# A per-sample 3x3 convolution on Trainium2: mixing every sample's taps from whole float32 weights instead of from weights split in two float16 parts

## The reference

```python
pooled = jnp.mean(x, axis=(2, 3))
att = sigmoid(pooled @ att_w.T + att_b)              # 16 samples x 4
agg_w = jnp.einsum('nk,kocij->nocij', att, weight)   # per sample 256 x 256 x 3 x 3
out = vmap(conv)(groupnorm(x), agg_w)                # padding 1, stride 1
return x + out
```

## Time and profile before

| | us |
|---|---|
| median of 3 runs | 1337.74 (1337.7 to 1338.12) |
| the profiled execution, its own time | 1337.87 |
| its span, first to last instruction | 1335.7 |
| PE busy | 1287.5 (96%) |
| DVE busy | 1209.1 (91%) |
| ACT busy | 916.6 (69%) |
| granted PE clock, mean | 0.997 of full speed |

### The profile page before, as it was taken

How to read it: one execution, slowest core, us unless ns; L and a number is a source line. 1 busy time by engine, 2 the same in 40 slices (tenths; PEclk the granted TensorE clock), 3 DMA queues, 4 the chain that set the end, 5 groups by cost and what they waited for, 6 DMA issues and landing times.

```text
span 1335.7 us, 22954 instructions
## 1 busy us (share of the span) xinstructions
PE 1287.5 (96%) x8596; PEld 731.8 (55%) x8596; DVE 1209.1 (91%) x2121; ACT 916.6 (69%) x1441; POOL 56.8 (4%) x72
## 2 busy tenths in 40 slices
PE   1899999999999999999999999999999999999998
PEld 0455555555555555555555555555555555555555
DVE  7988999999999999999999998999989999998983
ACT  4875767867667676676867767677776767667531
POOL 0000000000000000000000000000000000000000
PEclk9899999999999999999999999999999999999999
DMA  9214644446543555534455452555525255552434
GB/s 381 99 22 125 180 115 104 129 130 176 143 107 108 137 157 145 144 89 133 141 145 156 98 145 77 149 139 145 145 54 153 84 146 145 128 154 60 98 98 142
DMA packets 30475, 174.59 MB, mean 131 GB/s; under 512 B 3488, under 2 KB 3744, under 8 KB 28320
## 3 DMA queue, kind: packets, MB, share of 16 engines
q1 hardware_dynamic: 20288, 113.94, 23.1%
q0 software_dynamic: 8928, 49.78, 22.2%
q10 hardware_dynamic: 1152, 9.44, 2.2%
HBM read 112.33 MB, written 51.38 MB: 123 GB/s over the span
## 4 chain that ended last, share of the span: by engine, by line
PE 95%; issue 4%; DVE 1%; POOL 0%; POOLq 0%; DVEq 0%
PE pM L480 86%; PE pG L442 4%; PE pG L433 4%; PE pS L415 0%; DVE Us L655 0%; DVE E L642 0%; POOL small L1321 0%; DVE Vs L660 0%; DVE T L636 0%; POOL sel L1317 0%; DVE X L767 0%; DVE small L901 0%; DVE small L890 0%; DVE small L889 0%; DVE small L891 0%
## 5 line engine op out<-in xcount | busy, mean ns | idle before, releaser
L480 PE MATMUL pM<-Vs,Us 128*128 128x385 f16 (+1 forms) x6912 | 1160.2, 330 | 2.6 <-DVE Us L655 2.6
L480 PEld LDWEIGHTS pM<-Vs,Us 128*128 128x128 f16 x6912 | 673.5, 98 | 495.7 <-issue 23.2
L1026 ACT CAST Vs<-E 128x784 f16<-128x784 f32 x192 | 159.8, 840 | 137.3 <-DVE E L628 72.2
L603 DVE SCALAR_TENSOR_TENSOR T<-X 128x392 f32<-128x392 f32 x384 | 193.4, 560 | 12.2 <-ACT X L1081 10.5
L660 DVE TENSOR_TENSOR Vs<-E,Vs 128x784 f16<-128x784 f32 x192 | 182.9, 969 | 4.0 <-ACT Vs L1026 4.0
L628 DVE SCALAR_TENSOR_TENSOR E<-T 128x784 f32<-128x784 f32 x128 | 119.1, 972 | 2.2
L1041 ACT ACTIVATE Us<-E 128x768 f16<-128x768 f32 x120 | 95.9, 835 | 35.6 <-DVE E L642 35.6
L642 DVE SCALAR_TENSOR_TENSOR E<-G,T 128x768 f32<-128x768 f32 x128 | 117.0, 955 | 2.2
L1101 ACT ACTIVATE unused<-X,small 128x784 bf16<-128x784 f32 x120 | 113.8, 949 | 3.9
L1062 ACT ACTIVATE X<-pM,small 128x392 f32<-128x392 f32 x128 | 74.6, 583 | 59.3 <-PE pM L480 59.2
L655 DVE SCALAR_TENSOR_TENSOR Us<-E,Us 128x768 f16<-128x768 f32 x120 | 111.8, 952 | 0.1
(11 more groups left out here) (83 smaller groups left out, 646.9 us busy)
## 6 DMA issues: line engine op xcount, KB each, us to landing
X<-x_dram SPq DMA_DIRECT2D x66, 784.0 KB, 5.4
out_dram<-X SPq DMA_DIRECT2D x64, 784.0 KB, 3.8
X<-x_dram POOLq DMA_DIRECT2D x62, 784.0 KB, 8.1
W<-w_dram SPq DMA_DIRECT2D x8, 1152.0 KB, 19.7
G<-W ACTq DMA_DIRECT2D x8, 1152.0 KB, 5.6
attw<-attw_dram SPq DMA_DIRECT2D x1, 128.0 KB, 8.3
small<-attb_dram SPq DMA_DIRECT2D x1, 0.5 KB, 8.9
```

What stands on the lines that cost most here:

```text
L480: mm = pe.matmul(tile_rows(bank(k, o))[:, :, first:last], Us[:, j, a, c, o, kx, :], v_in(j, b, c, kx), start=(at < 2 and i == 0), stop=(i ...
L603: ins = dve.scalar_tensor_tensor(out=dst[c], in0=a[c], scalar=scale, in1=d[c], op0=ALU.mult, op1=ALU.add)
L1026: act.copy(v_out(j, 0), e_buf(n, ("V", chunk, j))).then_inc(v_hi, 1)
```

## The change

No piece is split any more: `SPLIT` becomes empty. `split_before(n)` is then empty for every n, so `mix_tile` issues only L433's float32 products in all 16 samples, and `attention` scales D32 in all of them. ACT's copy aside and high part, DVE's low part and PE's wait on `w_lo` in `mix` leave the program. The wait that the diff adds in `mix_tile` stands behind a condition on `split_in`, which is never met with an empty `SPLIT`.

```diff
-SPLIT = ((), (0,), (4,), (1,), (5,), (2,), (6,), (3,), (7,))
+SPLIT = ()
@@ mix_tile
                 if not is_first(n) or m >= MIX_BANKS:
                     pe.wait_ge(taps_taken, n * TAKES + m - MIX_BANKS + 1)
+                if not is_first(n) and m in (0, FULL):
+
+                    new = [i for i in split_in(n - 1) if m == FULL or i < JT]
+                    if new:
+                        pe.wait_ge(w_lo, len(split_before(n - 1)) + len(new))
@@ mix
                 if u == 0:
                     pe.wait_ge(att_ready, n + 1)
-                    if split_in(n - 1):
-                        pe.wait_ge(w_lo, len(split_before(n)))
@@ vector, epoch
                 add_rows(n, b, 3, 1)
-                if len(split_in(n)) > 0:
-                    w_low(n, 0)
@@ scalar, epoch
-                if split_in(n):
-                    w_aside_too(n)
                 take_pair(n, b, 3, 1)
                 if more:
                     sums(n + 1, 1 - b, 1, 1)
                 v_high(n, 1, 3)
-                if len(split_in(n)) > 0:
-                    w_high(n, 0)
```

## The result

The changed kernel takes 1342.26 us (median of 7 runs, 1342.05 to 1342.62), the kernel before 1338.09 us in the same comparison (1337.7 to 1338.88). The ratio is 1.0031, with an interval of 1.0019 to 1.0043: slower by 0.3%, by 4.2 us. The profiled execution has a span of 1340.3 us, 4.6 us above that of before.

The account below looks back on a forecast made before the run. The prediction took PE, busy for 96% of the span, to bound the kernel. Whole mixing's 15.4 us less the pauses' 11.1 us gave +4.3 us on 1337.74 us: 1342.0 us, range 1340.9 to 1344.5 us.

Parts of the forecast that it names:

- The pause, 11.1 us: Ahead of mixing samples 2 to 9, PE waits on `w_lo`; removing eight pauses gains 10.55 + 0.56 = 11.1 us.
- What is late next: At the mixing's start, nothing takes the pause's place; `att_ready` comes 2.2 us ahead of PE.
- DVE's gain: Freed of `w_low`, DVE waits for ACT's normalising and starts `v_pair` some 0.5 us ahead of the mixing; costed at nothing.
- The cover of 2 us for the U tiles: At point 3, DVE finishes the U pair 2 us before PE needs it, and later taps do not eat that.
- Whole against split mixing, 15.4 us: Whole mixing costs PE 14.0 us over samples 9 to 15 plus 1.4 us for the partly split samples.
- the 1.4 us of the partly split samples: Mixing of samples 2 to 8: splitting pays almost nothing until all four pieces of a tile are split; together 1.4 us.
- The periods: From one sample's mixing to the next, all periods become 80.6 us; about 1125.4 us from sample 1 to 15.
- Eviction as the bound (a): Rival: eviction bounds the mixing, float32 products cost nothing, only the pauses count; 1326.6 us, faster; chance 0.03.
- Relief of PE (b): Rival: relief of DVE, ACT and DMA speeds PE by a further 1.6 us or more; about 1340 us; chance 0.05.
- A later release (c): Rival: a later release, for instance `att_ready`, takes the pause's place, half of each left; 1347.4 us; chance 0.03.
- late U tiles (d): Rival: taps come later, DVE hands U on later than PE needs it; +4.6 us, 1346.6 us; chance 0.05.
- the inner bounds: In the sum: +4.0 us with 1.97 us a sample; +5.4 us with 2.07 us and pauses worth only 10.55.

Follow-up runs that it names:

- the run with the wait at its first use: Kernel before, but PE waits for a new split piece only ahead of the first tile that reads it; 1332.92 us, ratio 0.9963.
- three runs: Kernel before, splitting only pieces 0 to 3 (1336.64 us), only 0, 4, 1, 5 (1347.53 us), or all eight in order 0 to 7 (1335.16 us).
- the first run: Changed kernel with the old splitting work, written to unread space, and PE's wait on it put back; mixing stays whole; 1353.5 us.
- the fastest kernel: Kernel before with two pieces split in each of epochs 1 to 4, first mixing block and ACT's take moved; 1320.96 us, ratio 0.9872.

## Why the prediction was right

- **What bounds the kernel.** PE, in both kernels. That held: 16.4 us less work on DVE and 14.6 us less on ACT brought nothing but the end of the pauses.
- **The pause, 11.1 us.** Right in cause, and in size within half a microsecond. Put back alone it cost 11.2 us; half of it taken away, with the splitting kept, gave 1337.85 - 1332.92 = 4.9 us by the medians and 5.1 us by the spans (1335.7 against 1330.6), where 5.4 were expected; taken away entirely it gave 10.8 us. What I argued from two time stamps, 0.10 us between the low part's end and the mixing's start, the releaser named in the run with the wait at its first use has since confirmed.
- **What is late next.** Nothing, as said. In the kernel after, `att_ready` comes 2.2 us ahead of PE: D is scaled by 181.34 and the mixing starts at 183.50.

```profile
181.10 0.24 DVE L742 TENSOR_SCALAR D<-D,small 128x32 f32<-128x32 f32 x1
...
183.02 1.52 DVE L606 SCALAR_TENSOR_TENSOR T<-X 128x392 f32<-128x392 f32 x3 [0.73 <-ACT X L1082]
```

  The second row shows what was said of DVE's gain: freed of the low part it waits for ACT's normalising, 0.73 us, and starts its V pairs 0.5 us ahead of the mixing. The cover of 2 us for the U tiles held as well. Behind the mixing of sample 3, DVE is through with them (L658) at 300.64 in the kernel after, and PE, at 3.00 us a group from 284.54 on, comes to them at about 302.5: 1.9 us. In the kernel before it is 303.23 against 305.1 (six groups from 287.13 on), also 1.9 us. Later taps did not eat it, as argued.
- **Whole against split mixing, 15.4 us.** The run with the pauses put back has 15.65 us for it. The 2.00 us a sample are seen in the blocks of sample 13; the 1.4 us of the partly split samples rested on the rule that one whole piece holds up its tile, and three runs bear it out (1336.64, 1347.53 and 1335.16 us).
- **The periods.** 80.6 us predicted, 80.62 us found, early and late. The one from mixing 1 to mixing 2 is 77.63 us, about one group of 3.0 us shorter, since in the epoch of sample 0 the first block stands one group later; the prediction's "all periods 80.6 us" passes over it, though its 1125.4 us needs it. From mixing 1 to mixing 15 1125.4 us predicted, 1125.67 us found.
- **Rivals.** Eviction as the bound (a) would have made the kernel faster; PE's blocks grew by their full 2.0 us. Relief of PE (b) is excluded by 324 products in 53.99 us in both, and by the first run. A later release (c) and late U tiles (d) did not come: the profile after has PE's waits for DVE's D and Us in the start-up only. They were live risks, though: moving one block of 2.7 us uncovered a late release, on ACT's take, and the fastest kernel very likely waits 0.45 us for U tiles, the kind of (d).
- **Range.** The measured difference of medians, 4.2 us, is within 0.1 us of the 4.3; 1342.26 lies 0.3 us above the 1342.0, because the kernel before stood at 1338.09 in the comparison and not at 1337.74. The bounds of 1340.9 to 1344.5 were wider than the terms needed; they covered hidden waits, of which none came. The sums for the inner bounds are slightly off: with 1.97 and 2.07 us a sample they come to +4.1 and +5.3 us, not +4.0 and +5.4, and the rows do not show where these two readings come from. Nothing rests on them at a measured 4.2 us. A part of the close agreement is luck: counted from the mixing of sample 1 to the end, with the start-up left out, the two terms are 15.7 and 11.3 us (1245.63 us with the pauses put back, 1229.97 before, 1234.36 after), and their small errors of 0.3 and 0.2 us partly cancel.

## What to carry to other kernels

When a trace holds both regimes that a change chooses between, read the price of the change as the difference of two periods, and check it by a second view. Before removing work because of the wait that it causes, ask whether the wait can go alone: here the work was worth 15.4 us and its wait 11.1, and moving one block and one take kept the one without the other. Here a conversion done piece by piece paid only once the last member of a group that runs side by side was converted; where a trace shows the same, order the pieces by groups.

## What the runs showed of the hardware

Four products side by side in the array, float32 and float16 mixed, took nearly as long here as four float32 ones: 8.34 us for a sample with half of the pieces split, 8.38 us with none, 6.38 us with all. A block of three whole tiles takes 2.72 us where three float16 products for each of its pieces take 2.06 us. A pause of 1.36 us in each period left the granted clock at 1.00 in that period. A wait of 0.2 us in each of eight epochs did not appear as idle time of PE; it showed only as 0.41 us of idle time of the weight loads and in the length of the period, and it went when ACT's take was moved.
